# First layers of a ViT tower on one core: squares, roots and exponentials regrouped, the complex weights split in three parts, the second half's softmax placed around the first queries

## The reference, cut to what matters

```python
h = tokens(x)                                   # (8, 66, 192)
n = layernorm(h)
qr, qi, kr, ki, v = heads(n @ W.T for W in ...) # 12 heads of 16
sr = (qr kr' + qi ki') / 4 ; si = (qi kr' - qr ki') / 4
h = h + softmax(sqrt(sr*sr + si*si)) @ v
x = layernorm(h)
for i in range(4):                              # encoder, 12 heads of 64
    nx = rmsnorm(x) ; q, k, v = nx @ Wq, nx @ Wk, nx @ Wv
    x = x + softmax(q k' + bias) @ v @ Wo
    nx = rmsnorm(x)
    x = x + relu(nx @ Wi) @ Wo2 (+ experts in layers 1 and 3)
out = h + rmsnorm(x)
```

## Time and profile before

| | us |
|---|---|
| median of three runs | 741.36 |
| the profiled execution | 745.19 |
| its span in the trace | 743.4 |
| PE busy | 678.4 (91%) |
| DVE busy | 446.8 (60%) |
| ACT busy | 405.0 (54%) |
| POOL busy | 351.7 (47%) |

### The profile page before, as it was taken

The page is one execution under the profiler, slowest core; times in us unless marked ns, Lnnn a source line. Parts: engine busy times, 40 slices in busy tenths (PEclk is TensorE's granted clock), DMA queues, the critical chain, the costliest instruction groups (busy, mean ns, idle before and its releaser), DMA issues.

```text
span 743.4 us, 16264 instructions
## 1 busy us (share of the span) xinstructions
PE 678.4 (91%) x6658; PEld 609.8 (82%) x6658; DVE 446.8 (60%) x941; ACT 405.0 (54%) x914; POOL 351.7 (47%) x329
## 2 busy tenths in 40 slices
PE   6879979799889999999899989998899999999995
PEld 4757857588768888999899878787688898999994
DVE  0483567275475677565566655853856775666664
ACT  1486655534364374776675455444543647767642
POOL 2755275742573561547674424426734514553510
PEclk9998779988999999999999999989999999999998
DMA  9210100400221122434444110002211124333200
GB/s 256 75 48 7 40 1 2 118 2 1 77 74 44 33 72 64 134 109 128 134 118 122 42 45 2 2 1 75 76 44 33 61 75 134 90 104 107 75 1 23
DMA packets 36769, 49.20 MB, mean 66 GB/s; under 512 B 6315, under 2 KB 27735, under 8 KB 36183
## 3 DMA queue, kind: packets, MB, share of 16 engines
q1 hardware_dynamic: 33259, 43.49, 20.3%
q10 hardware_dynamic: 3436, 4.67, 2.1%
HBM read 47.70 MB, written 0.45 MB: 65 GB/s over the span
## 4 chain that ended last, share of the span: by engine, by line
PE 63%; DVE 11%; ACT 9%; POOL 8%; DMA 4%; issue 3%; ACTq 1%; SPq 0%; POOLq 0%; DVEq 0%
PE pd L716 31%; PE pa L716 21%; PE ps L716 7%; PE pa L747 4%; POOL prob L649 3%; POOL w L640 3%; ACT wide L1057 2%; DMA gate<-in_gate_w_dram 2%; DVE xn L1143 1%; DVE mx L1097 1%; ACT pa L1058 1%; DVE prob L1265 1%; POOL prob L655 1%; DVE xs L1109 1%; DVE xs L1107 1%
## 5 line engine op out<-in xcount | busy, mean ns | idle before, releaser
L640 POOL TENSOR_TENSOR w<-raw,w 128x384 fp32r<-128x384 f32 x140 | 141.7, 1014 | 126.3 <-ACT w L968 118.4
L716 PE MATMUL pd<-wide,w 128*128 128x264 f32 x1200 | 157.8, 288 | 0.1
L716 PEld LDWEIGHTS pd<-wide,w 128*128 128x128 f32 x1200 | 151.0, 190 | 1.0 <-DVE wide L1288 0.9
L716 PE MATMUL pa<-xs,w 128*128 128x264 f32 x810 | 121.2, 290 | 12.3 <-DVE wide L1288 8.1
L716 PEld LDWEIGHTS pa<-xs,w 128*128 128x128 f32 x810 | 107.7, 191 | 16.8 <-DVE wide L1288 10.2
L1288 DVE TENSOR_TENSOR wide<-pa,wide 128x264 fp32r<-128x264 f32 x144 | 62.0, 432 | 42.3 <-ACT pa L1058 40.2
L649 POOL TENSOR_TENSOR prob<-prob,mx 66x792 f32<-66x792 f32 x36 | 54.3, 1511 | 57.4 <-DVE mx L1097 57.1
L1057 ACT ACTIVATE wide<-pa 128x264 fp32r<-128x264 f32 x144 | 56.9, 395 | 38.1 <-PE pa L716 38.0
L655 POOL TENSOR_TENSOR prob<-prob,rc 66x792 f32<-66x792 f32 x36 | 54.3, 1511 | 45.1 <-DVE rc L1103 45.1
L716 PE MATMUL ps<-xs,w 128*128 128x264 f32 x480 | 74.2, 285 | 0.6 <-DVE prob L1265 0.6
L1179 DVE TENSOR_TENSOR pd<-pd,vtok 128x264 f32<-128x264 f32 x64 | 43.6, 681 | 41.5 <-PE pd L716 41.3
(11 more groups left out here) (139 smaller groups left out, 1101.0 us busy)
## 6 DMA issues: line engine op xcount, KB each, us to landing
raw<-in_moe_w_dram SPq DMA_DIRECT2D x16, 576.0 KB, 4.1
raw<-in_moe_w_dram SPq DMA_DIRECT2D x16, 384.0 KB, 3.5
raw<-in_moe_w_dram SPq DMA_DIRECT2D x32, 192.0 KB, 4.0
vtok<-cw_rows ACTq DMA_DIRECT2D x4, 1056.0 KB, 6.1
raw<-in_attn_o_dram SPq DMA_DIRECT2D x4, 576.0 KB, 4.0
raw<-in_ffn_wo_dram SPq DMA_DIRECT2D x4, 576.0 KB, 4.1
vtok<-in_patches_dram SPq DMA_DIRECT2D x2, 768.0 KB, 7.9
raw<-in_attn_q_dram SPq DMA_DIRECT2D x4, 384.0 KB, 3.8
```

The source lines that it names most:

```text
L640: ins = nc.gpsimd.tensor_tensor(low, whole, high.bitcast(F32), ALU.subtract)
L716: return nc.tensor.matmul(out_ap, lhsT, rhs, start=first, stop=last)
```

## The change

It only moves work, apart from the number of dummy products and the cutting of one copy and one subtraction in three.

- The complex weights: high and low part in three pieces of 768 columns; PE waits for the piece that it needs. The wait for the small loads stands in front of ACT's first `cproj` copy.
- Chunk 2 (the value weights of layer 0) has a landing place of its own, `raw_third`, and is loaded at the start with chunks 0 and 1; its high part (`high`) is made ahead of the first `cscores`, its low part (`low`) after `cpv` of image 2.
- First half: four `cscores`, then four `croot`, then the exponentials; `cscores` of the second half's first image moves in between the first half's `cpv`.
- Second half: `croot` 2 and 3 stand between queries and keys, `v` of image 1 ahead of the first `ctp`, and `cpv` one place later; `v` of image 2 stands before the last `ctp`.
- End of the second half: `tp` and `pv` of layer 0's image 0 and the `scale` stand before `scores` of image 3.
- The split of `w1` stands between queries and keys of half 1, that of `w2` after `scores_end` of half 1.
- Dummy products: 6, 6 become 4, 4; 2 and 1 more before and behind the first `ctp`; 2 becomes 1 before and 2 becomes 4 after the norm of half 0; 4, 3, 3 become 3, 2, 2.

```diff
     yield ("cproj", 0, 1)
     yield ("cproj", 0, 2)
+    yield ("high", None, "qkv", 0, 2)
     for b in range(HALF_B):
         yield ("cscores", 0, b)
-        if b:
-            yield ("croot", 0, b - 1)
         yield ("cvals", 0, b)
-    yield ("croot", 0, HALF_B - 1)
+    for b in range(HALF_B):
+        yield ("croot", 0, b)
     yield ("cproj", 1, 0)
-    yield from warm(6)
+    yield from warm(4)
     yield ("cexp", 0, 0)
     yield ("cexp", 0, 1)
     yield ("cproj", 1, 1)
-    yield from warm(6)
+    yield from warm(4)
     yield ("cexp", 0, 2)
+    yield ("cexp", 0, 3)
+    yield ("cproj", 1, 2)
+    yield from warm(2)
     yield ("ctp", 0, 0)
-    yield ("cexp", 0, 3)
-    yield ("sqrt_table", None)
-    yield ("cproj", 1, 2)
+    yield from warm(1)
+    yield ("ctp", 0, 1)
     yield ("cpv", 0, 0)
-    yield ("ctp", 0, 1)
+    yield ("cscores", 1, 0)
+    yield ("ctp", 0, 2)
+    yield ("cpv", 0, 1)
     yield ("cvals", 1, 0)
-    yield ("cpv", 0, 1)
-    yield ("ctp", 0, 2)
     yield ("cvals", 1, 1)
+    yield ("ctp", 0, 3)
     yield ("cpv", 0, 2)
-    yield ("ctp", 0, 3)
+    yield ("low", None, "qkv", 0, 2)
     yield ("cvals", 1, 2)
     yield ("cvals", 1, 3)
     yield ("cpv", 0, 3)
+    yield ("sqrt_table", None)
     yield ("mean", 0, "encoder")
-    yield ("split", None, "qkv", 0, 2)
-    yield from warm(2)
+    yield from warm(1)
+    yield ("cscores", 1, 1)
     yield ("squares", 0, "encoder")
-    yield ("cscores", 1, 0)
     yield ("norm", 0, "encoder", 0)
-    yield ("cscores", 1, 1)
-    yield from warm(2)
+    yield ("croot", 1, 0)
+    yield from warm(4)
     yield ("scale", 0, "ln1", 0)
-    yield ("croot", 1, 0)
+    yield ("croot", 1, 1)
     yield ("cscores", 1, 2)
-    yield ("croot", 1, 1)
     yield ("scale", 0, "encoder", 0)
     yield ("cscores", 1, 3)
-    yield from warm(4)
+    yield from warm(3)
     for layer in range(LAYERS):
         last = blocks_of(layer) - 1
         if layer not in MOE_LAYERS:
             if layer == 0:
                 yield ("qk", 0, 0, 0)
-                yield ("qk", 0, 0, 1)
                 yield ("croot", 1, 2)
                 yield ("croot", 1, 3)
+                yield ("qk", 0, 0, 1)
                 yield ("scores", 0, 0, 0)
                 yield ("cexp", 1, 0)
                 yield ("cexp", 1, 1)
                 yield ("v", 0, 0, 0)
                 yield ("cexp", 1, 2)
                 yield ("cexp", 1, 3)
+                yield ("v", 0, 0, 1)
                 yield ("ctp", 1, 0)
                 yield ("scores", 0, 0, 1)
+                yield ("ctp", 1, 1)
                 yield ("cpv", 1, 0)
-                yield ("ctp", 1, 1)
-                yield ("v", 0, 0, 1)
+                yield ("ctp", 1, 2)
                 yield ("cpv", 1, 1)
-                yield ("ctp", 1, 2)
+                yield ("v", 0, 0, 2)
+                yield ("ctp", 1, 3)
+                yield ("cpv", 1, 2)
                 yield ("scores", 0, 0, 2)
-                yield ("cpv", 1, 2)
-                yield ("ctp", 1, 3)
-                yield ("v", 0, 0, 2)
                 yield ("cpv", 1, 3)
                 yield ("mean", 1, "encoder")
+                yield ("v", 0, 0, 3)
                 yield ("squares", 1, "encoder")
-                yield ("v", 0, 0, 3)
                 yield ("norm", 1, "encoder", 0)
+                yield ("tp", 0, 0, 0)
+                yield from warm(2)
+                yield ("scale", 1, "ln1", 0)
+                yield ("pv", 0, 0, 0)
                 yield ("scores", 0, 0, 3)
-                yield ("tp", 0, 0, 0)
-                yield from warm(3)
-                yield ("scale", 1, "ln1", 0)
+                yield ("scale", 1, "encoder", 0)
+                yield ("tp", 0, 0, 1)
                 yield ("scores_end", 0, 0)
                 yield ("split", None, "o", 0, 0)
-                yield ("pv", 0, 0, 0)
-                yield ("scale", 1, "encoder", 0)
-                yield ("tp", 0, 0, 1)
-                yield from warm(3)
+                yield from warm(2)
                 yield ("pv", 0, 0, 1)
                 early = 2
...
-            yield from qk(1, layer)
+            yield ("qk", 1, layer, 0)
             if layer == 0:
-                yield from split_block(0, 0)
+                yield ("split", None, "w1", 0, 0)
+            yield ("qk", 1, layer, 1)
             for b in range(HALF_B):
                 yield from warm(2)
                 if b >= early:
@@ -211,6 +214,8 @@
             yield ("pv", 1, layer, 0)
             yield ("tp", 1, layer, 1)
             yield ("scores_end", 1, layer)
+            if layer == 0:
+                yield ("split", None, "w2", 0, 0)
             yield ("o_main", 0, layer)
...
                 nc.sbuf_tensor("csq", [S, 2, 2, 3, 2 * S], F32) as csq, \
-                nc.sbuf_tensor("probT_late", [S, 2, HG, S], F32) as probT_late:
+                nc.sbuf_tensor("probT_late", [S, 2, HG, S], F32) as probT_late, \
+                nc.sbuf_tensor("raw_third", [128, 2 * F], F32) as raw_third:
...
-        chunks = [x[2:] for x in order if x[0] == "split"]
+        chunks = [x[2:] for x in order if x[0] in ("split", "high")]
...
-            load(0)
-            load(1)
+            for c in range(3):
+                load(c)
             sp.wait_ge(d_free, groups_after(D_GROUPS, ("bias", 0)))
             sp.dma_start(bias_rows, bias_cols[:, :]).then_inc(bias_stored, 16)
             sp.wait_ge(bias_stored, 16)
             sp.dma_start(bias[:, :, :], bass.AP(bias_rows.tensor, 0, [[1, S], [2 * S, H], [1, S]])).then_inc(bias_loaded, 16)
 
-            for c in range(2, len(chunks)):
+            for c in range(3, len(chunks)):
                 sp.wait_ge(chunk_split, c - 1)
...
-            pool.wait_ge(cx_hi, 1)
-            nc.gpsimd.tensor_tensor(wcx[1], rawcx[:, :, :], wcx[0].bitcast(F32), ALU.subtract).then_inc(cx_split, 1)
+            for part in range(3):
+                cols = slice(part * 2 * D, (part + 1) * 2 * D)
+                pool.wait_ge(cx_hi, part + 1)
+                nc.gpsimd.tensor_tensor(wcx[1][:, :, cols], rawcx[:, :, cols], wcx[0][:, :, cols].bitcast(F32),
+                                        ALU.subtract).then_inc(cx_split, 1)
             for stage in order:
                 name = stage[0]
-                if name == "split":
+                if name in ("split", "low"):
                     low_parts()
...
-                        if hf == 0:
-                            pe.wait_ge(cx_split, 1)
+                    if hf == 0:
+                        pe.wait_ge(cx_split, stage[2] + 1)
                     for m in range(3 * stage[2], 3 * stage[2] + 3):
...
-            nc.scalar.activation(wcx[0], rawcx[:, :, :], ACT.Copy).then_inc(cx_hi, 1)
-            act.wait_ge(in_small, 16 * SMALL_LOADS)
-            nc.scalar.activation(wvc_sb[:, 1, :], wvc_sb[:, 1, :], ACT.Copy, scale=0.5).then_inc(small_ready, 1)
-            nc.scalar.activation(gate[:, :, 1, :], gate[:, :, 1, :], ACT.Copy, scale=0.5).then_inc(small_ready, 1)
+            for part in range(3):
+                cols = slice(part * 2 * D, (part + 1) * 2 * D)
+                nc.scalar.activation(wcx[0][:, :, cols], rawcx[:, :, cols], ACT.Copy).then_inc(cx_hi, 1)
             for at, stage in enumerate(order):
                 name, hf = stage[0:2]
                 if name == "cproj":
+                    if hf == 0 and stage[2] == 0:
+                        act.wait_ge(in_small, 16 * SMALL_LOADS)
+                        nc.scalar.activation(wvc_sb[:, 1, :], wvc_sb[:, 1, :], ACT.Copy, scale=0.5).then_inc(small_ready, 1)
+                        nc.scalar.activation(gate[:, :, 1, :], gate[:, :, 1, :], ACT.Copy, scale=0.5).then_inc(small_ready, 1)
                     for j in range(3):
...
-                elif name == "split":
+                elif name in ("split", "high"):
                     high_part()
```

More of the change, by code:

```diff
@@ L453, in vit_tower @@
         in_vec, bias_stored, bias_loaded = sem("in_vec"), sem("bias_stored"), sem("bias_loaded")
-        raw_loaded = [sem("raw_loaded0"), sem("raw_loaded1")]
+        raw_loaded = [sem("raw_loaded0"), sem("raw_loaded1"), sem("raw_loaded2")]
         cx_hi, cx_split = sem("cx_hi"), sem("cx_split")
@@ L539, in probs, with slot_of, raw_of @@
             return prob_late[:, u - HALF_B] if HALF_B <= u < B else prob[:, u % HALF_B]
+        def slot_of(c):
+            return 2 if c == 2 else c % 2
+        def raw_of(c):
+            return raw_third[:, :] if c == 2 else raw[:, c % 2, :]
         def chunk_places(c):
             kind, layer, i = chunks[c]
-            slot = raw[:, c % 2, :]
+            slot = raw_of(c)
             if rows_in(kind):
@@ L568, in load @@
                 src = chunk_source(kind, layer, i)
-                slot = raw[:, c % 2, :]
+                slot = raw_of(c)
                 if rows_in(kind):
                     dst = slot.rearrange("p (a n) -> p a n", a=2)
```

(18 more changed lines are left out.)

## The result

The changed kernel takes 738.79 us (median of 20 runs, 731.55 to 743.69), the kernel before in the same comparison 741.77 us (20 runs). The ratio is 0.9949 with a 95% interval of 0.9928 to 0.9970: faster by 0.5%, 3 us by the medians where 14 were forecast, and the median lies above the range's 736.5. Two later comparisons of the same two kernels gave 0.9932 (0.9908 to 0.9955) and 0.9943 (0.9907 to 0.9979). By the three ratios the gain is 4 to 5 us, by the medians 3 to 6.

A forecast was written before the change was run, and what follows sets the result against it. TensorE, busy 91% of the span, was taken to lose time to four waits and the half clock after some. Gains of 6.2 up to half 1's queries and 7.6 after make 13.8, say 14.0 us: median 727.4, range 719.5 to 736.5.

The forecast's parts named there:

- Steps A to C: Start to queries of half 0: gain 1.1 us at the start, cumulative 3.0 after the first half's softmax, 2.9 at the queries.
- D: Second half's roots between queries and keys of half 0: first transpose 1.75 us sooner, cumulative 4.65, PE idle 4.93 to 1.6.
- the bound: First half's softmax: most that the moved low part on POOL could cost beside DVE's additions, 2.4 us; 0.3 counted.
- Step E: Second half's cpv to queries of half 1: net 3.1, cumulative 7.7; scale 1.2 more, 8.9; 2.7 paid back, 6.2.
- the first wait: Second half's last cpv: its addition queues behind DVE's addition, maximum and sum for scores of image 2, costing 3.2 us.
- The stall in the queries: Queries of half 1: PE fills three banks and waits about 2.7 us behind DVE's scaling, pv and ACT's copies.
- new waits bite: Rival: clock falls at the pause before half 1's queries, w2 delays the norm, POOL clashes; 6.4 less, 733.8 us; chance 0.17.
- Step F: Half 1's queries to FFN: splitting w1 and w2 apart removes PE's 4.75 us idle and half clock; net 7.6 us.
- The last step, from one execution to the median: Whole kernel: profiled execution lies 3.8 us above the median of 741.36, so 731.2 profiled means a median of 727.4.
- everything shifts: Behind layer 0: nothing changes and all later work comes earlier by the sum of the gains, 14.0 us.
- all stages behind 180 shifted by the same 14: Sign of success: every stage after 180 us comes earlier by the same 14 us.

The follow-up runs named there:

- squares_only: The changed kernel with the squares of half 1 before the values of image 3, scores of image 2 left in place; 735.31 us, 0.9921.
- squares_first: The changed kernel with scores of image 2 before the values of image 2, and squares of half 1 before the values of image 3; 728.08 us, 0.9783.
- before_third: The kernel before, unchanged, run again for a third trace; the trace's span is 737.1 us.
- before_w1_w2_apart: The kernel before with only w1's split moved between queries and keys of half 1 and w2's after scores_end; 736.72 us, 0.9937.
- after_third: The changed kernel, unchanged, run again for a third trace, on another chip; 736.37 us, 0.9943.
- after_w1_w2_together: The changed kernel with w1 and w2 split in one go behind the keys again; 742.05 us, 1.0023.
- dummies_norm0: The changed kernel with 9 dummy products in PE's pause between the second half's cscores of image 1 and the norm of half 0; 739.74 us, 0.9979.
- scores_earlier_old_tail: The changed kernel with scores of image 2 before its values, and the kernel before's order from mean of half 1 to pv of image 1; 728.10 us, 0.9809.
- after: The changed kernel's first profiled trace, span 733.4 us; the kernel measured 738.79 us, 0.9949 against the kernel before.

## Why the prediction was wrong

**Steps A to C held, by the trace they were made from, and D in part.** The squares start at 20.56 (20.6 forecast), the function set is loaded at 47.69 (47.5), POOL multiplies from 51.55 (51.45), the mean of half 0 comes at 64.66 (64.8), the queries at 79.6 (80.1), PE's idle time before the second half's first transpose is 1.65 us (1.6), and the transpose comes at 95.2 (94.8). The last agreement has some luck in it: from the queries to the transpose it takes 15.6 us where 14.7 were forecast, and the queries come 0.5 us early. The moved low part did clash, but less than the bound. POOL in the changed kernel:

```profile
57.45 4.65 POOL L654 TENSOR_TENSOR wqkv<-raw_third,wqkv 128x384 fp32r<-128x384 f32 x4
```

DVE beside it:

```profile
57.91 2.25 DVE L1263 TENSOR_TENSOR vtok<-csq 66x396 f32<-66x396 f32 x2 [1.47 <-ACT csq L1040]
```

Two additions took 2.25 us instead of 1.14 (two of 0.57) and POOL itself 4.65 instead of 4.4; `cpv` of image 1, queued behind them, was added at 60.08, and the mean came when forecast.

**Step E failed, between the mean of half 1 and its queries.** Up to the mean it held: 107.25 measured, 107.0 forecast (114.67 less the 7.7), with the first wait sized at 3.2 us and measured at 2.83. From there to the queries the kernel before takes 11.75 us. I took 1.2 off for the moved `scale`, 10.5 in all; measured were 17.8. The queries start at 125.06 instead of 117.5 and end at 134.8 instead of 127.7, later than the 133.97 of the kernel before. What I left out is the moved pair `v`, `squares`. In my own terms, of a moved stage I had read the PE part and not what it queues ahead of on ACT, and I let the clock stay up in this stretch. With this pair put back, squares_only and squares_first both take 10.6 us, the forecast of the term. Of the 7.2 us between, 1.1 is PE's wait for the squares; the rest goes with the low clock in this stretch. The stall in the queries, 2.7 us forecast, is not in the changed kernel, where PE comes to them 7 us later; in these two it is 2.80 and 2.79.

That the queries of squares_first end at 128.1, within 0.4 us of the 127.7, is luck. It does not have the first wait that the forecast had counted, so its mean comes 1.6 us earlier, and the clock falls inside its queries, which the forecast did not have.

The rival "new waits bite" named the clock and nearly this place. It let the clock fall at the stall inside the queries, for 3 us. In squares_only and squares_first a low stretch does follow that stall, but 1 minus the granted clock sums to only 1.7 us over it. In the changed kernel the clock was low before, from 108 to 129, for a sum of 8.5 us (1.7 and 6.8), and there is no such stall.

**Step F held in place and nearly in size.** The idle time at 141 is gone, PE has 1.00 from 134 to 176, and w2's instructions stand in front of the power as forecast (159.97 to 163.08 on POOL, the power at 163.08). From the queries' end to the FFN the profiled pair went from 41.5 to 32.5 us, 9.0 against 7.6 forecast. But a part of this is the stretch at 169 to 177, which the kernel before has in two of three traces only. Against before_third, which does not have it and takes 39.3 us, before_w1_w2_apart (32.5) wins 6.9 us, and so does after_third against after_w1_w2_together (32.5 and 39.3). The ratios give 4.7 us for step F alone, and 5.5 to 7 for its removal.

**The last step, from one execution to the median, failed too.** The forecast subtracted one gain from the median. The kernel before has executions with five low stretches (FFN at 175.5) and with two (170.0); the terms of steps B, C and F were read from one with five. The 2.9 us of steps A to C at the queries in particular exist only against those: before_third has its queries at 78.5, all changed traces at 79.6 to 80.5, since the new order has a low stretch at 70 to 83 in every trace without the dummy products of dummies_norm0, behind the 2.04 us for which PE waits until ACT has squared. I had that pause in the sum and kept the low stretch for both kernels, where one of them has it only sometimes. Behind layer 0, "everything shifts" is true of the order and not of the time: from the FFN to the end the traces above take 563.3 to 571.9 us, for the same list of stages. So the sign "all stages behind 180 shifted by the same 14" failed too. Where the later low stretches lie differs from trace to trace, and the 10 us of the profiled pair are the 8.2 us up to the FFN plus 1.8 of this.

Two readings of my own were off without changing the outcome. The page has 0.7 in two of the first eleven slices, not in four; three more have 0.8. And the terms of step E's first part, 3.45 + 3 - 3.2, give 3.25 and not 3.1.

What stays open: which property of the light stretches lets the clock fall. Filling an idle time of 2 to 3 us moved the stretches and shortened the run in none of three kernels; the pause of 2.83 us was followed by a low stretch in the three changed traces, in dummies_norm0 and in after_w1_w2_together, and not in squares_only. And why step F gives 7 to 9 us in the traces up to the FFN and 5 to 7 over all executions is argued from the spread behind layer 0, not shown.

The best version, squares_first at 728.08 us, is 2.2% faster than the kernel before (0.9783). Against the changed kernel it is 1.1% by the medians on one chip (736.37), and 1.5 to 1.7% by the ratios of both against the kernel before (0.9932 to 0.9949); scores_earlier_old_tail equals it at 728.10.

## What to carry to other kernels

When a stage moves in a list that all engines share, go through its part on every engine: `v` moved ahead of `squares` looked like filler for PE and was two copies in front of a critical square on ACT, in a stretch where the clock then fell as well. Before adding up gains from a trace, take the trace of the unchanged kernel two or three times: a gain against a stretch at half clock is real only if that stretch is there every time. And an order that removes waits beat dummy products placed into them: 8 us by the medians (728.08 against 736.37 on one chip) against none.

## What the runs showed of the hardware that I had not expected

- The granted clock differs between executions of one kernel in the same places: 1 minus the mean granted clock, times the span, was 27.5, 24.0 and 17.3 us in three traces of the kernel before, and single stretches cost 1.7, 3.4 or 5.1 us.
- Two low stretches hardly 3 us apart (108 to 112, 115 to 129) came out within 2 us of the same places in all three traces of the changed kernel. Of those behind 200 us, one lay at 477 to 484 in after and at 259 to 267 in the other two.
- Twelve dense products directly ahead of this stretch delayed the drop from 108 to 115 us (one trace) and did not prevent it.
- A low stretch needs no long idle time of PE just before it: in the kernel before the clock is low from 169 to 177 with PE busy throughout, and from 153 to 169 PE's longest idle time is 0.99 us. It came in two of three traces.
